# A recommendation tower on one core: late weights packed and loaded at the start, weight folding and dense layer done early, three engines' call orders laid anew

## What is computed

```python
e = jnp.stack([tbl_f[ids[:, f]] for f in range(26)], axis=1)      # 512 x 26 x 64
x = layer_norm(dense_t @ Wd.T, gd, bd)                            # 512 x 128
y = layer_norm(einsum('bnd,ed->bne', e, Ws), gs, bs)
y = layer_norm(einsum('bne,pn->bep', y, Wsi), gsi, bsi)           # over p
T = concatenate([x[:, None, :], swapaxes(y, 1, 2)], axis=1)       # 33 items of 128
Z = einsum('bnd,bmd->bnm', T, T)                                  # lower triangle: 528
z = layer_norm(Zflat @ Wl.T, gl, bl)[:, :384]
h = maximum(concatenate([z, dense_t]) @ W_top1 + b_top1, 0)       # 512 x 512
h = maximum(h @ W_top2 + b_top2, 0)                               # 512 x 256
out = h @ W_top3
```

## Time and profile before

| | |
|---|---|
| median of 3 runs | 216.56 us (216.52 to 218.41) |
| span of the profiled execution, first to last instruction | 181.1 us |
| what lies around the span (216.56 less 181.1) | 35.5 us |
| PE busy | 151.1 us (83%) |
| DVE busy | 119.6 us (66%) |
| POOL busy | 108.4 us (60%) |
| ACT busy | 79.6 us (44%) |
| mean granted TensorE clock | 0.942 |
| moved by DMA | 9.76 MB |

### The profile page before, as it was taken

How to read it: one execution, slowest core, us unless ns; L and a number is a source line. 1 busy time by engine, 2 the same in 40 slices (tenths; PEclk the granted TensorE clock), 3 DMA queues, 4 the chain that set the end, 5 groups by cost and what they waited for, 6 DMA issues and landing times.

```text
span 181.1 us, 3314 instructions
## 1 busy us (share of the span) xinstructions
PE 151.1 (83%) x1189; PEld 103.9 (57%) x1189; DVE 119.6 (66%) x325; ACT 79.6 (44%) x221; POOL 108.4 (60%) x139
## 2 busy tenths in 40 slices
PE   0248294998979999499998979999999999789894
PEld 0147142744646667356556767665987564485683
DVE  0702667685789567949868598994689798857300
ACT  3101220442786455445345546442636634651251
POOL 1877877777777777777777777777774003620000
PEclk9999755589999999789999999999999999999999
DMA  5411199311111112331111233111113200000000
GB/s 179 161 22 29 22 297 380 81 34 23 29 27 29 29 22 53 74 73 29 25 29 24 47 73 79 29 26 28 31 25 73 51 18 0 2 4 0 0 0 0
DMA packets 9729, 9.76 MB, mean 54 GB/s; under 512 B 3665, under 2 KB 7377, under 8 KB 9458
## 3 DMA queue, kind: packets, MB, share of 16 engines
q0 software_dynamic: 3328, 3.41, 9.7%
q1 hardware_dynamic: 5954, 5.18, 9.2%
q10 hardware_dynamic: 432, 0.97, 1.6%
HBM read 7.98 MB, written 0.00 MB: 44 GB/s over the span
## 4 chain that ended last, share of the span: by engine, by line
PE 58%; DVE 16%; POOL 9%; DMA 5%; ACT 5%; issue 5%; ACTq 0%
PE pz L487 10%; POOL emb L380 8%; PE pc L451 8%; PE py L472 7%; PE pf L503 6%; PE tu L434 5%; DVE y_ms L1091 3%; DMA emb<-tables_dram,rows_at 3%; PE pf L522 3%; PE tu L424 3%; PE py L467 3%; DVE T L1100 2%; PE pf L549 2%; PE py L503 2%; PE pf L529 2%
## 5 line engine op out<-in xcount | busy, mean ns | idle before, releaser
L380 POOL DMA_INDIRECT emb<-tables_dram,rows_at x104 | 100.3, 964 | 31.5 <-issue 30.9
L451 PEld LDWEIGHTS pc<-wbd,emb 128*128 128x128 f32 x128 | 20.2, 201 | 16.8 <-issue 13.7
L451 PE MATMUL pc<-wbd,emb 128*128 128x192 f32 (+4 forms) x128 | 28.5, 333 | 1.2 <-DVE emb L1085 1.2
L487 PE MATMUL pz<-T 128*64 128x67 f32 x512 | 22.5, 230 | 6.6 <-DVE T L1100 5.5
L487 PEld LDWEIGHTS pz<-T 128*64 128x64 f32 x512 | 18.1, 138 | 14.6 <-DVE T L1100 7.4
L1091 DVE TENSOR_REDUCE y_ms<-ysq 128x16 f32<-128x512 f32 x32 | 20.4, 679 | 7.3 <-ACT ysq L772 7.3
L757 ACT ACTIVATE embT<-tu 128x256 f32<-128x256 f32 x26 | 9.9, 380 | 32.6 <-PE tu L424 32.6
L424 PE MATMUL tu<-proj_w,emb 128*128 128x128 f32 x52 | 12.8, 316 | 10.4 <-DMA emb<-tables_dram,rows_at 10.3
L1100 DVE TENSOR_TENSOR T<-py,y_r 128x512 f32<-128x512 f32 x32 | 20.6, 687 | 0.5
L772 ACT ACTIVATE ysq<-py 128x512 f32<-128x512 f32 x32 | 17.3, 594 | 6.8 <-PE py L472 6.6
L434 PE MATMUL tu<-mbd,embT 128*128 128x128 f32 x104 | 18.3, 303 | 0.5 <-ACT embT L757 0.5
(11 more groups left out here) (142 smaller groups left out, 203.2 us busy)
## 6 DMA issues: line engine op xcount, KB each, us to landing
emb<-tables_dram,rows_at POOLq DMA_INDIRECT x104, 2.4
z<-gram SPq DMA_DIRECT2D x48, 32.0 KB
w<-w_dram SPq DMA_DIRECT2D x1, 1280.0 KB
wl<-wl_dram SPq DMA_DIRECT2D x1, 1024.0 KB
denseT<-denseT_dram ACTq DMA_DIRECT2D x1, 512.0 KB, 4.8
w<-w_dram SPq DMA_DIRECT2D x1, 512.0 KB
comb_w<-comb_w_dram ACTq DMA_DIRECT2D x1, 311.0 KB, 3.4
sel<-sel_dram SPq DMA_DIRECT2D x1, 240.0 KB, 5.0
```

The costliest lines, as they stand in the source:

```text
L380: pool.indirect_dma_start(emb[:, 2 * pair + half, :], None, t["tables"], bass.IndirectOffsetOnAxis(ap=rows_at[:, 2 * g + half, j:j + 1], a ...
L451: mm = pe.matmul(PC[m % NPC][:, :, :].rearrange("p b c -> p (b c)")[:, col:col + n], of, wbd[:, :, :].rearrange("p b c -> p (b c)")[:, at: ...
L487: mm = pe.matmul(PZ[2 * PR * h:2 * PR * h + 2 * PR, ITEMS * b:ITEMS * (b + 1)], of[:, 0:2 * PR], of, start=True, stop=True)
```

## The change

The late weights are packed (small ones into one tensor `small_w`; `wlx` with `gbsi`; `wdT` with `denseT`; `w1` split in two) and are all issued at the start, without the wait for a gather. POOL's memsets move ahead of the first gather. `folded_weights` writes into bank PY[0] and `dense_layer` into PY[1] and PZ by turns, in place of PF; both stand near the start of PE's list. The tick loops are replaced by lists of calls that are written out for PE, ACT and DVE.

```diff
             sp.dma_start(index_parts[:, :], t["index_parts"]).then_inc(l_ids, 16)
             sp.dma_start(proj_w[:, :], t["proj_w"]).then_inc(l_proj, 16)
+            sp.dma_start(small_w[:, :], t["small_w"]).then_inc(l_small, 16)
             sp.dma_start(bias9[:, 0:E], t["bs"].partition_broadcast(P)).then_inc(l_nine, 16)
-            sp.dma_start(sel9[:, :, :], t["sel9"]).then_inc(l_nine, 16)
-            sp.wait_ge(gathered[5], 32)
-            for dst, src in ((wl, "wl"), (wlx, "wlx"), (gb, "gb"), (sel, "sel"), (gbsi, "gbsi"), (mask, "mask"),
-                             (glbl, "glbl"), (w1, "w1"), (b1, "b1"), (w2, "w2"), (b2, "b2"), (w3, "w3")):
-                sp.dma_start(dst[tuple(slice(None) for _ in dst.shape)], t[src]).then_inc(l_late, 16)
+            sp.dma_start(wlx_gbsi[:, :], t["wlx_gbsi"]).then_inc(l_small, 16)
+            sp.dma_start(wl[:, :, :], t["wl"]).then_inc(l_wl, 16)
+            sp.dma_start(w1[:, KEPT // P:, :], t["w1_dense"]).then_inc(l_dense1, 16)
+            sp.dma_start(mask[:, :], t["mask"]).then_inc(l_late, 16)
+            sp.dma_start(w1[:, 0:KEPT // P, :], t["w1_flat"]).then_inc(l_late, 16)
+            sp.dma_start(w2[:, :, :], t["w2"]).then_inc(l_late, 16)
...
             act.dma_start(comb_w[:, :], t["comb_w"]).then_inc(l_comb, 16)
-            act.dma_start(wdT[:, :, :], t["wdT"]).then_inc(l_dense, 16)
-            act.dma_start(denseT[:, :, :], t["denseT"]).then_inc(l_dense, 16)
+            act.dma_start(dense_w[:, :, :], t["dense_w"]).then_inc(l_dense, 16)
...
+            pool.memset(T[:, :, ITEMS - 1:ITEMS], 1.0).then_inc(consts_ready, 1)
+            pool.memset(fold[:, :, :], 0.0).then_inc(consts_ready, 1)
+            pool.memset(foldx[:, :], 0.0).then_inc(consts_ready, 1)
...
+            pool.wait_ge(consts_ready, 10)
             pool.wait_ge(l_ids, 16)
...
-            gather(range(6))
-            pool.memset(T[:, :, ITEMS - 1:ITEMS], 1.0).then_inc(consts_ready, 1)
-            pool.memset(fold[:, :, :], 0.0).then_inc(consts_ready, 1)
-            pool.memset(foldx[:, :], 0.0).then_inc(consts_ready, 1)
...
-            gather(range(6, STEPS))
+            gather(range(STEPS))
...
+        def fold_bank():
+            return PY[0][:, :, :].rearrange("p b c -> p (b c)")
+
+        def dense_bank(m):
+            return [PY[1][:, :, :].rearrange("p b c -> p (b c)"), PZ][m % 2]
...
             def dense_layer(m):
                 if m == 0:
-                    pe.wait_ge(l_late, 16 * 12)
-                    pe.wait_ge(wl5_ready, 1)
-                wait_if_any(pe, d1_ready, m)
+                    pe.wait_ge(l_dense1, 16)
+                    pe.wait_ge(l_dense, 16)
+                if m == 1:
+                    pe.wait_ge(sc_ready, 1)
+                wait_if_any(pe, d1_ready, m - 1)
...
             def folded_weights():
                 pe.wait_ge(fold_ready, 1)
-                pe.wait_ge(xs_ready, 1)
+                pe.wait_ge(l_wl, 16)
...
+                    pe.wait_ge(wl5_ready, 1)
+                    pe.wait_ge(d1_ready, H1 // P - 1)
...
+                if m == 0 and half == 0:
+                    pe.wait_ge(d1_ready, H1 // P)
...
+            u_sums(25)
+            merge(2)
+            y_sums(14)
+            scale_rows(25)
+            normalise(14)
+            y_sums(15)
+            z_stats(2)
+            normalise(15)
+            z_normalised(2)
```

More of the change, by code:

```diff
@@ L736, in _ @@
-            mlp1_rest(last, 3)
-            mlp2(last)
-            mlp3(last)
+                    pe.matmul(fold_bank()[0:ROWS_X, :], fold[:, k, :], wl[:, k, :], start=(k == 0), stop=False)
+                pe.matmul(fold_bank()[0:ROWS_X, :], foldx[:, :], wlx, start=False, stop=True).then_inc(w5_done, 1)
+            bias_sums()
+            spread_matrix()
+            transposes(0)
+            folded_weights()
+            x_projected()
+            spread_products(0)
+            dense_layer(0)
@@ L1220, in _ @@
[L1220 to L1227 removed]
+            centre_wsi()
+            centre_ws()
+            place(0)
+            gamma_weights()
+            place(1)
+            place(2)
+            place(3)
+            place(4)
+            place(5)
+            place(6)
@@ new lines, in _ @@
+            place(7)
+            place(8)
+            fold_weights()
+            bias_parts()
+            centre_wd()
+            place(9)
+            place(10)
+            place(11)
+            place(12)
+            u_sums(0)
+            x_normalised()
+            scale_rows(0)
+            u_sums(1)
+            u_sums(2)
+            scale_rows(1)
+            scale_rows(2)
+            u_sums(3)
+            y_sums(0)
+            scale_rows(3)
+            normalise(0)
+            u_sums(4)
@@ new lines, in _ @@
+            linear_features(0, 1)
+            scale_rows(10)
+            linear_features(0, 2)
+            y_sums(5)
+            linear_features(0, 3)
+            normalise(5)
+            u_sums(11)
+            scale_rows(11)
+            u_sums(12)
+            scale_rows(12)
+            y_sums(6)
+            normalise(6)
+            u_sums(13)
+            merge(0)
+            scale_rows(13)
+            y_sums(7)
+            normalise(7)
+            u_sums(14)
+            scale_rows(14)
@@ new lines, in _ @@
+            z_stats(0)
+            z_normalised(0)
+            y_sums(8)
+            linear_features(1, 0)
+            linear_features(1, 1)
+            linear_features(1, 2)
+            linear_features(1, 3)
+            u_sums(15)
+            normalise(8)
+            scale_rows(15)
+            u_sums(16)
+            scale_rows(16)
+            first_layer_sums(0)
+            u_sums(17)
+            y_sums(9)
+            scale_rows(17)
+            normalise(9)
+            u_sums(18)
@@ new lines, in _ @@
+            merge(1)
+            scale_rows(18)
+            y_sums(10)
+            normalise(10)
+            u_sums(19)
+            scale_rows(19)
+            z_stats(1)
+            z_normalised(1)
+            y_sums(11)
+            normalise(11)
+            u_sums(20)
+            u_sums(21)
+            scale_rows(20)
+            scale_rows(21)
+            u_sums(22)
+            first_layer_sums(1)
+            scale_rows(22)
+            linear_features(2, 0)
+            linear_features(2, 1)
```

834 lines of the change are left out of this document (475 added, 359 removed).

## The result

The changed kernel takes **239.33 us** (median of 5 runs, 235.04 to 242.33), the kernel before 218.41 us (median of 5, 216.52 to 221.77). The forecast was 211.2 us, and its range ended at 217.5.

The account below looks back on a forecast made before the run. POOL's gather pace (5.04 us a quad) and PE were taken as close limits in the middle, with a chain behind the last quad. Span 181.1 - 5.4 = 175.7, plus 35.5 carried over, gave 211.2 us; 8-in-10 range 208.5 to 217.5.

Parts of the forecast that it names:

- the term carried over: Difference between the profiled span (181.1 us) and the runs' median (216.56): 35.5 us, added unchanged to the forecast span.
- The forecast's gain: spread_products(25) 5.4 us sooner: 1.25 memsets, 2.4 work taken from before it, the rest PE's lag behind the gathers.
- Step 1: POOL's memsets ahead of the gathers: later gathers come 1.25 us sooner, the last issued at 135.6.
- Step 2: All loads at the start: they end at about 16.5 us, and transposes(0) ends at 15.8, bounds 12.4 and 17.
- Rival C: Start: two load queues hold up the first gathers by 6.8 us; time 211.8 us; chance 0.05.
- Step 3: Early folding and dense layer: combine(0) at 28.3 us, transposes(6) at 47.4 against 47.98, POOL not held up.
- Step 4: Middle, transposes(6) to (25): 82.2 us busy, 7.0 idle; POOL's pace then sets transposes(25), taken at 139.4.
- rival B: Middle: ACT and DVE orders stall PE 10 us instead of 7, transposes(25) at 142; 213.8 us; chance 0.17.
- Step 5: End: spread_products(25) at 140.1 instead of 145.47, then 15.5 us to the last gram copy's end, last 20.1 unchanged.
- A: Start stays at the low clock, POOL waits 5.4 us from 35.1 on; 216.8 to 217.3 us, or 220; chance 0.18.
- the last sign of being wrong: New profile: a changed difference between span and time would fault the 35.5 us carried over.

Follow-up runs that it names:

- before_again: The kernel before, unchanged, profiled once more: 219.15 us, with a span of 218.8.
- new_start_by_sp: The change up to about quad 8, the order of before behind it, rows copied by SP's plain DMAs instead of gathers (lookup left out): 174.17 us.
- rows_by_sp_old: The changed kernel's loads, packing and memsets with the old call order and banks, rows copied by SP's plain DMAs (lookup left out): 179.51 us.
- after_ahead26: The changed kernel with QUADS_AHEAD = 26 instead of 3, so that POOL never waits for PE: 296.87 us, ratio 1.3913.

## Why the prediction was wrong

**The base failed first.** "The runs' median of 216.56 is 35.5 us more, which I carry over unchanged." The sum rested on a span that no timed run has. The 35.5 us don't lie around the span (1.9 us do), and they are not a constant: `before_again` has them as late increments, and they grow with another order. With its rows brought by SP and no increment late the change takes 181.93 us. The forecast on such a base was 175.7 of span and 1.9 around it, 177.6, so 4.3 us of the miss of 28.1 are the sum's own (0.6, if the rows come by POOL's plain DMAs, 178.16). The other 23.8 are what the term carried over was too small by: 33.6 us (35.5 less 1.9) were in the sum, and 57.4 (239.33 less 181.93) is what the gathers add.

The forecast's gain did not come either. It put 5.4 us, 1.25 of them from the memsets; without late increments the change is 2.4 us slower than the old order with the same loads and memsets (179.51), so the order lost where it was to gain 4.

**Step 1, memsets: right in itself.** The 13th gather starts 15.87 us behind the first instead of 17.09, and the forecast was 1.25 us less. The last is issued at 181.00 instead of 135.6, for POOL's waits further on.

**Step 2, loads: right.** The second transpose of quad 0 ended at 15.4 us in the changed kernel (forecast 15.8, bounds 12.4 and 17), and the loads fill the first three slices of 5.9 us. Rival C would have had it at 19.2, and that does not show.

**Step 3, early folding: right where no increment is late.** The clock in 19 to 36 us is 1.00 instead of 0.54; `x_projected` ends at 24.2 (forecast 24.1).

```profile
19.00:36.00 17.00, 13.84 (x65) 8.59 (x64) 5.53 (x17) 7.32 (x23) 10.92 (x12) 1.00 0.11 21
```

But "POOL is not held up" failed at once: the product of `transposes(1)` ended at 26.18, 0.3 us behind POOL's asking, its increment came 2.0 us after that, and POOL's next gather started at 28.44 behind 2.84 us of waiting. The forecast had looked at `transposes(3)`, `(4)` and `(6)` only. By its own terms `transposes(1)` ends near 26.5 (24.1, and 0.65 for the spread products, 1.4 for a dense layer, 0.35 for itself), and POOL asks for it near 25.3 (5.10 + 4 x 5.04), so it should have put a wait of about 1 us there. `combine(0)` came at 31.04 instead of 28.3, `transposes(4)` at 46.5 instead of 38. The start itself gains: `new_start_by_sp` is 5.3 us faster than `rows_by_sp_old` (174.17 against 179.51). That this is nearly the forecast's 5.4 is chance, since both have the memsets' gain and neither has the new end, of which the forecast was made. With gathers the gain is not seen (1.0034).

**Step 4, the middle: failed.** From `transposes(6)` to `(25)` I put 82.2 us busy and 7.0 idle, 89.2. Without late increments it is 97.1, 85.7 busy and 11.4 idle:

```profile
46.03:143.15 97.12, 85.69 (x812) 60.23 (x810) 75.11 (x197) 48.03 (x134) 0.00 (x0) 0.98 0.17 40
```

The idle time is rival B's (10 us), and the work 3.5 us more than I counted. The granted clock there is 0.98 as before, so the 1.6 us that I took off for a stretch at 1.2 GHz did not come. The idle time stands before these two groups (us and who ended it, at the end of the line):

```profile
L465 PE MATMUL pc<-wbd,emb 128*128 128x192 f32 (+4 forms) x95 | 17.8, 319 | 5.6 <-DVE emb L1267 5.6
L448 PE MATMUL tu<-mbd,embT 128*128 128x128 f32 x76 | 12.6, 291 | 3.1 <-ACT embT L860 3.1
```

PE comes to a combine before `scale_rows` is done, and to spread products before the copy of the transposes is. I had kept the 7.0 us of idle time without a reason from the new lists. Before, these two groups had 1.2 and 0.0 us of it. The old lists behind the new start need 87.2 (46.76 to 134.00 in `new_start_by_sp`). With gathers the same stretch takes 145 us in the changed kernel (from 55.2 to 200.67), where POOL's pace would allow 96.

**Step 5, the end: right.** `spread_products(25)` stands 0.9 us behind `transposes(25)` instead of 3.1. From its start to the end of the last gram copy it is 15.58 us (201.58 to 217.16), forecast 15.5, and from there to the end 20.4, forecast 20.1. The same distance behind a `transposes(25)` that comes at 200.67 is worth nothing.

**The rivals.** A had the sign and not the mechanism: the clock was high and POOL was held up all the same. None of the rivals held that the page of before was itself the odd execution, although I had its number before me: 16% between span and time. Only the last sign of being wrong named it, a changed difference between span and time, and that sign came. Two small slips change nothing: rows 3 give 3.60 us for the eight passes that I read as 3.4, and A's sum comes to 216.6 to 217.1, not 216.8 to 217.3.

## What to carry to other kernels

Set the span of a profiled execution against the timed runs first. If the two are far apart, no sum on that page is worth its terms, and the difference is where to look. Where a kernel gathers with indirect DMAs on POOL beside PE, don't count a product as delivered at its end, and don't let POOL run freely ahead without timing it (QUADS_AHEAD = 26 cost 33% in the old order). An order of calls is to be timed beside such gathers, since one that is 2.4 us worse without them was some 18 us worse with them.

## What the hardware did that I had not expected

- PE's semaphore increments come late while POOL issues indirect DMAs: 70 of 140 in the kernel before, 41 of 140 in the changed one, by 0.4 to 12 us, and up to 43 and 65 us where POOL never pauses. With plain DMAs from POOL or SP, or with memsets on POOL: 0 of 150.
- They come in bunches: at 28.0 us four of them, whose products had ended 2.0 to 3.8 us before. And they outlast the gathers: in both kernels with QUADS_AHEAD = 26 the last late ones came 15 us behind the last gather.
- In `after_ahead26` the first eleven late ones, from 32.85 to 146.25 us, lie whole multiples of 0.70 us apart, as if something let them through in turn. What that is no run shows.
- The same products are late each time: 35 of the 41 in the changed kernel were late again in its second profile.
- One execution of the kernel before, the one whose page was shown, had none late with the same gathers (0 of 148, span 181.1). No timed run of that kernel was like it (212.4 to 222.2 us beside the experiments). Why it was spared is open: the indirect DMAs were in every case of late increments, but they are not enough for them. The page that was spared also has nearly all records of DVE's updates (282 of 287, where `before_again` has 189), and so have the runs without gathers; whether the lost records and the late increments have one cause, or the recording a part in them, no run here tells. Open too is whether the products themselves or only their increments are late, since the ends of matmuls in a trace are modelled.
- PE's granted clock falls with the holes: 0.57 in 22 to 135 us of `after_ahead26`, where PE is busy 20.5 us of 113, 0.95 in 150 to 250 (87.5 of 100), and 1.00 over the span of `new_start_by_sp`.
- Memsets of 128x960 on POOL raised DVE's busy time from 119.2 to 131.6 us, and not by slowing all of it: some short operations lasted up to 0.95 us, the time of a memset (0.90), while their median stayed at 0.17 to 0.18.
